# Path copies of the backward pass moved from GpSimd to ScalarE, and the path's stores split one to seven between SyncE and ScalarE

## What is computed

```python
D = _pairwise_euclidean(small, large)      # small: 722 context rows, large: 100 rows of x
R = _dtw_cost(D)                            # r[i,j] = D[i,j] + min(up, left, diag)
i_idx, j_idx, valid = _backtrack(R, T_small, T_large)
contrib = small[i_idx] * valid[:, None]
expanded = zeros((T_large, d)).at[j_idx].add(contrib)
...
x = x + align(ctx_1024, layernorm(x))
x = x + moe(layernorm(x))                  # 16 experts, 3 of them for each row
x = x + cross_attention(ctx_1024, layernorm(x), mask)
x = x + lora_ffn(layernorm(x))
```

## Time and profile before

| | |
|---|---|
| median of 3 runs | 1289.1 us (1288.01 to 1289.37) |
| the profiled execution | 1289.95 us |
| its span | 1288.3 us |
| busy, share of the span | PE 84%, DVE 37%, ACT 25%, POOL 18% |
| `warp` from the first backward step (195.9 us) to the next stage's first instruction (305.0 us) | 109 us |
| POOL copies of the path | 5, of about 3.5 us |
| ACT copies of the path | 4, of 3.45 to 0.6 us |
| stores of the path | 4 on SP, 4 on ACT |

### The profile page before, as it was taken

One profiled execution on the slowest core, in us unless ns is written; L12 is line 12 of the kernel. 1 busy time (PEld: TensorE's weight loads), 2 busy tenths in 40 slices (PEclk: granted clock), 3 DMA queues, 4 the chain that ended last, 5 costly groups with the idle time before them and its releaser, 6 DMA issues. The chain is left out here.

```text
span 1288.3 us, 16885 instructions
## 1 busy us (share of the span) xinstructions
PE 1086.2 (84%) x5214; PEld 691.1 (54%) x5215; DVE 480.2 (37%) x1700; ACT 326.4 (25%) x799; POOL 226.3 (18%) x320
## 2 busy tenths in 40 slices
PE   5775679932945999999999999498999779999997
PEld 5773234520425767667767767244466464555553
DVE  4656888883562000001000001256545363112112
ACT  4323665541000222222222222233355220000000
POOL 0834031430002112121211121100000001111111
PEclk9897899965975999999999999798999958999999
DMA  8488004124612485765696665420000070000000
GB/s 283 126 169 260 20 1 166 55 92 93 231 39 80 153 290 171 269 206 187 197 334 197 202 204 175 130 76 0 1 1 1 2 271 1 1 1 6 20 1 26
DMA packets 76424, 152.53 MB, mean 118 GB/s; under 512 B 17690, under 2 KB 21914, under 8 KB 75566
## 3 DMA queue, kind: packets, MB, share of 16 engines
q1 hardware_dynamic: 63390, 131.46, 30.1%
q0 software_dynamic: 6928, 17.04, 6.0%
q10 hardware_dynamic: 6048, 3.33, 1.2%
HBM read 131.57 MB, written 20.25 MB: 118 GB/s over the span
## 5 line engine op out<-in xcount | busy, mean ns | idle before, releaser
L1270 ACT ACTIVATE att<-phid,b 128x128 f32<-128x128 f32 x216 | 79.4, 368 | 308.5 <-PE phid L1239 308.5
L1292 DVE TENSOR_TENSOR att<-py,att 128x512 f32<-128x512 f32 x27 | 18.7, 692 | 369.7 <-PE py L1247 369.7
L1239 PEld LDWEIGHTS phid<-tiles,W 128*128 128x128 f32 x896 | 111.5, 192 | 37.4 <-issue 37.4
L1239 PEld LDWEIGHTS phid<-tiles,Wmem 128*128 128x128 f32 x832 | 105.9, 196 | 38.9 <-issue 38.9
L1239 PE MATMUL phid<-tiles,W 128*128 x896 | 114.4, 276 | 1.1 <-issue 0.3
L1239 PE MATMUL phid<-tiles,Wmem 128*128 x832 | 108.8, 280 | 5.5 <-issue 4.5
L1247 PE MATMUL py<-W,att 128*128 128x512 f32 x224 | 110.0, 593 | 0.0
L1247 PE MATMUL py<-Wmem,att 128*128 128x512 f32 x208 | 102.2, 593 | 0.0
L2101 PE MATMUL acc<-hs,WoT 128*128 128x400 f32 x256 | 95.7, 518 | 0.5 <-POOL hs L2005 0.5
L2061 PE MATMUL bf<-xT_f,Wmem 128*128 128x400 f32 x256 | 93.7, 511 | 0.0
L2202 DVE SCALAR_TENSOR_TENSOR h<-bf,wb 128x400 f32<-128x400 f32 x64 | 34.0, 570 | 151.1 <-PE bf L2085 145.9
(11 more groups left out here) (365 smaller groups left out, 1675.1 us busy)
## 6 DMA issues: line engine op xcount, KB each, us to landing
Wmem<-in_W SPq DMA_DIRECT2D x16, 2048.0 KB, 14.1
W<-in_W SPq DMA_DIRECT2D x16, 2048.0 KB, 9.2
cT<-in_ctxT SPq DMA_DIRECT2D x8, 1444.0 KB, 11.4
ctx_rows<-in_ctx SPq DMA_DIRECT2D x8, 1280.0 KB
Wmem<-in_Wkv SPq DMA_DIRECT2D x2, 2048.0 KB, 9.0
att<-in_b SPq DMA_DIRECT2D x16, 256.0 KB, 14.1
Wmem<-in_WiT SPq DMA_DIRECT2D x1, 4096.0 KB
WoT<-in_WoT SPq DMA_DIRECT2D x1, 4096.0 KB
```

The lines of the kernel that those rows point to most:

```text
L1239: ins = pe.matmul(ph[j % NH][:, :], W1[u][:, k, j * P:(j + 1) * P], xgT[:, bass.ds(w, 1), k * P:(k + 1) * P].rearrange("p o t -> p (o t)") ...
L1270: act.activation(hT[:, j, :], ph[j % NH][:, :], ACT.Relu, bias=b1[:, bass.ds((e + u) * HJ + j, 1)]).then_inc(relu_ok, 1)
```

## The change

All nine pieces are copied by ScalarE. The five that GpSimd had are put into ScalarE's periods 3, 4, 6, 7 and 8, between `keep_keys_T` and `scale_keys`; the last four stay at the end of ScalarE's stream. In `route`, SP stores the path of batch 0 alone and ScalarE's queue stores batches 1 to 7. The work itself (shapes, bytes, number of transfers) stays the same.

```diff
-        POOL_COPY = (3, 4, 6, 7, 8)
+        COPY_IN = (3, 4, 6, 7, 8)
...
                 keep_keys_T(act, p - 3)
+            if p in COPY_IN:
+                keep_path(act, COPY_IN.index(p))
             if 0 <= p - 2 < B:
                 scale_keys(act, p - 2)
...
-        def keep_path(eng, copy, i):
+        def keep_path(act, i):
             q0, q1 = copies[i]
-            eng.wait_ge(scanned_r, ST - q0)
-            copy(path[:, :, q0:q1].rearrange("p a s -> p s a"), walk[:, q0:q1, NC - 2:0:-2]).then_inc(path_ok, 1)
+            act.wait_ge(scanned_r, ST - q0)
+            act.copy(path[:, :, q0:q1].rearrange("p a s -> p s a"), walk[:, q0:q1, NC - 2:0:-2]).then_inc(path_ok, 1)
...
                     invert(pool, p - 2)
-                if p in POOL_COPY:
-                    keep_path(pool, pool.tensor_copy, POOL_COPY.index(p))
...
-            for i in range(len(POOL_COPY), len(copies)):
-                keep_path(act, act.copy, i)
+            for i in range(len(COPY_IN), len(copies)):
+                keep_path(act, i)
...
         @block.sync
         def _(sp):
-            for b in range(0, B, 2):
-                store_path(sp, b)
+            store_path(sp, 0)
...
         @block.scalar
         def _(act):
-            for b in range(1, B, 2):
+            for b in range(1, B):
                 store_path(act, b)
```

## The result

The changed kernel takes 1275.18 us (median of 4, 1273.05 to 1276.62), the kernel before beside it 1289.23: ratio 0.9894, 95% interval [0.9882, 0.9907], 14.05 us less. The forecast was 1276.2.

The account below looks back on a forecast made before the run. VectorE's chain of 115 backward scans was taken to bound the kernel, held up by five GpSimd copies. 1289.95 - 12.1 - 0.8 = 1277.05, or 1276.2 us against the median 1289.1; range 1274.5 to 1280.6.

Parts of the forecast that it names:

- the twelve microseconds: VectorE's backward chain: five instructions lengthened beside GpSimd's five path copies lose 12.1 us together, which the change removes.
- The alternative cost of 15.6 us by full blocking: VectorE blocked for each whole GpSimd copy: five losses of 3.13 us, 15.6 us, changed kernel at 1272.7 instead of 1276.2.
- The same copy on ScalarE does not slow VectorE: Backward pass: the five stalls go and nothing takes their place, -12.1 us on VectorE.
- The rival that the stalls move with the copies: VectorE is slowed by any copy out of the memory it writes: about 1289, no difference; chance 0.04.
- The copies hide in ScalarE's periods: Copies of 3.45 us are covered by the wait for GpSimd's inversion and by TensorE's room: cost 0.
- 0.2 us of lateness for TensorE: Period 3: scaling ends at most 0.2 us later than TensorE wants it; periods 4 and 6 have the same spacing.
- 1.8 were forecast: Period 8, without products to cover the copy: TensorE turns the scaled keys 1.8 us later.
- The 0.6 us of lateness: The keys' work: periods 3, 4 and 6 together delay it by at most 0.6 us.
- the last inversion: GpSimd's last inversion, no longer behind its copy, starts 1.0 us earlier, at about 274.55.
- The room: ScalarE may reach its last four copies as late as 284.0 without cost, against 281.1 expected: 2.9 us.
- The stores: Start of the next stage: SP's first load goes 0.8 us earlier, issue to widening stays 4.6 us; gain 0.8 us.
- The rival that the load waits for all seven: Next stage: first load lands only after ScalarE's last store, losing 3.45 us, time 1280.5; chance 0.10.

Follow-up runs that it names:

- the run with other data: Changed kernel, with GpSimd also copying 128 x 736 elements between memory nobody else touches in its old five periods: 1285.8 us, ratio 0.9988.
- the repeat of the kernel before: The kernel before, run once more unedited: 1288.67 us, ratio 1.0004.
- the run with two more copies: Changed kernel, with ScalarE copying two of the pieces once more in period 8: 1276.72 us, ratio 0.9915.
- the later-stores run: Changed kernel, with ScalarE storing batches 2 to 7 only once the first load of the path has landed: 1278.41 us, ratio 0.9931.
- the added products, 28 and 36: Changed kernel, with small TensorE products of overwritten results at the next stage's start: 1272.65 us with 28, 1270.1 us with 36.
- the stores alone: Kernel before, with only the stores changed to one on SP and seven on ScalarE, copies still on GpSimd: 1286.33 us, ratio 0.9986.
- the copies alone: Changed kernel with the stores of before, four to four, all nine copies on ScalarE: 1274.95 us, ratio 0.9895.
- the two repeats: Changed kernel run again unedited: 1274.83 us, ratio 0.9902; and again beside the run with 28 added products: 1273.7 us, ratio 0.9891.

## Why the prediction was right, step by step

**What bounds.** VectorE's chain did, and the twelve microseconds were the five long instructions: 12.0 measured, 12.1 forecast. The price, from VectorE's rows and not from the copies' durations, was right: the copies of 3.5 us cost 2.4 each. The alternative cost of 15.6 us by full blocking is excluded: five would have shortened the pass to 91.4 us. The whole stage ran 4.4 us earlier than the absolute times of the forecast, since the backward pass began at 191.5 and not at 195.9; with that shift its last scan (286.5 for 290.9) and the next stage's start (288.6 for 292.9) came as forecast.

**The same copy on ScalarE does not slow VectorE.** Right, and now also with TensorE and DMA busy: nine copies, and no scan over 0.45 us. The rival that the stalls move with the copies is excluded, and the run with other data shows that it had the wrong cause.

**The copies hide in ScalarE's periods.** Right. I had summed durations and got 0.2 us of lateness for TensorE; the instructions overlap a little (the copy starts at 219.48, before the turned keys' 219.01 + 0.64, the scaling 2.99 us after it), so the turn was not late at all. In period 8 it was, by 1.2 us more of waiting (4.20 for 2.97), where 1.8 were forecast. The last turned keys ended 85.7 us after the first backward scan, where 281.1 - 195.9 = 85.2 were forecast, but that closeness is partly luck. The first turned keys came 27.5 us after the first scan instead of 25.7, a difference between executions, and from them to the last it took 57.6 us instead of 59.3: 1.7 us less, where 1.0 - 0.6 = 0.4 were forecast. The 0.6 us of lateness did not come about, and the last inversion came 1.7 us earlier instead of 1.0. In the repeat of the kernel before the same stretch took 57.8 us, so most of the 1.7 belongs to the one execution that the forecast was read from. The room, forecast as 2.9 us, was 3.1 by the run with two more copies; more than the forecast could know, it differs from execution to execution.

**The stores.** The mechanism was right and the term too small. The load went out 0.7 us sooner as forecast (0.8), but from its issue to the widening there were 4.0 us instead of the 4.6 that I carried over: 1.35 us for 0.8. Fewer stores were in its way, as the later-stores run shows: 2.9 us from issue to widening with one store beside it. ScalarE's seven stores took 6.29 us, not 8.05. The rival that the load waits for all seven is excluded: the last of them was issued at 294.0 and no store landed in under 3.5 us, so it was still on its way at 297.5, and the widening came at 296.46.

**Not foreseen.** 0.7 us between the first widening and the table products. TensorE's first path products in the kernel before (the changed kernel's are above), and its granted clock, the third number from the end, in stretches of one microsecond of the kernel before and then of the changed one:

```profile
314.98 13.32 PE L996 MATMUL px<-ctx_rows,cost_mem 128*100 128x512 f32 x24 [34.10 <-DVE cost_mem L1054]
```
```profile
319.00:320.00 1.00, 1.00 (x2) 0.29 (x1) 0.00 (x0) 0.00 (x0) 0.00 (x0) 0.50 0.61 112
320.00:321.00 1.00, 1.00 (x3) 0.45 (x2) 0.00 (x0) 0.00 (x0) 0.00 (x0) 0.69 0.91 117
```
```profile
300.00:301.00 1.00, 1.00 (x2) 0.37 (x2) 0.00 (x0) 0.00 (x0) 0.00 (x0) 0.50 0.73 141
301.00:302.00 1.00, 1.00 (x3) 0.34 (x2) 0.00 (x0) 0.00 (x0) 0.00 (x0) 0.97 0.73 144
```

Before, the products began at 314.98 and the clock rose from 0.50 to 1.00 about 5.6 us later; in the changed kernel it rose about 3.9 us after 297.14. That this moment wanders without the change is shown: 4.8 us in the repeat of the kernel before, and 5.6 and 3.7 us after the first of the added products, 28 and 36 of them. Whether the 0.7 us are the change's doing or chance is open. By the table the stretch takes 78.0 and 77.6 us before, 78.0 with the stores alone, 77.6 with the copies alone, 77.3 and 77.1 in the changed kernel: too close together to tell.

**The sum.** -12.0 and -1.35, and up to -0.7, make 13.4 to 14.1; measured 14.05, and 13.2 and 14.3 in the two repeats. Of this the stores' part, 1.1 to 1.4 us, stands in the traces of every kernel that has them, while whole times hardly tell: copies alone 1274.95 and both together 1274.83.

## What to carry to other kernels

If one engine runs a long chain of short dependent steps, list its instructions that last much longer than their median, and look at what GpSimd starts at those moments. Here five GpSimd copies of 3.5 us each cost 12 us of 107, and the cure was to put the same copies on an engine that had waits of its own to put them in. Price the move by the waits of the receiving engine, and look at them in more than one execution: here they were 2.4 us in one and 5.8 in another. Then count everything in the queue behind a transfer that you delay: 6 us later for stores that nobody waited for made a load late which stood behind fourteen others in the queue.

## What the runs showed of the hardware

A GpSimd copy of 128 x 736 elements holds up VectorE instructions with two inputs in SBUF (scan, `scalar_tensor_tensor`) by 2.3 to 2.5 us of its 3.3 to 3.5; they end 0.4 to 0.6 us before the copy does in the profile. A memset of the same elements holds nothing up, nor does GpSimd's inversion of 128 x 8 elements in 1.7 us. The shuffles with one input were never long, also those that start 0.1 us after a copy, but they last only 0.15 us; no run has a long one-input instruction there. ScalarE's copy of 128 x 736 bf16 elements into strided places takes 3.45 us, 4.7 ns for each element of a partition, and a GpSimd memset of as many elements, also written with a stride, 3.27 us, so the writing alone costs GpSimd about as much as the copy. TensorE's clock fell to half (1.2 of 2.4 GHz) at 266.9 us in the changed kernel, when after the products of period 7 (ended at 262.4) only turns and head sums were left, and rose 2.7 (run with later stores) to 5.6 us (kernel before) after the path's products began; products whose result nobody uses raise it as well (3.7 and 5.6 us).
